# Weighted sum of attention values in a four-layer graph network: group updates in pieces, shared roots, and a mark on ScalarE

## What is computed

```python
h = jnp.maximum(_layernorm(x, axis=-1), 0.0)
x = x + _L0_gnn_ref(h, src, dst, ...)     # inside it:
    e = jnp.exp(score - smax[dst])
    m = v[src] * (e / ssum[dst])[:, :, None]
    t = jax.ops.segment_sum(m, dst, num_segments=N).reshape(N, DIM)
    new_h = (t @ Wa + ba) * alpha + h * (1.0 - alpha)
h = jnp.maximum(_layernorm(x, axis=-1), 0.0)   # needs the inverse root of each node's variance
```

## Time and profile before

| | us |
|---|---|
| median of three runs | 10655.52 |
| profiled execution | 10607.1 |
| its span, first to last instruction | 10605.0 |
| weighted sum, first L1063 to last L1063 | 1544.9 to 1901.9 |
| busy in the span: PE, DVE, ACT, POOL | 5675.4, 3028.2, 949.0, 6216.3 |

### The profile page before, as it was taken

How to read it: one execution, slowest core, us unless ns; L and a number is a source line. 1 busy time by engine, 2 the same in 40 slices (tenths; PEclk the granted TensorE clock), 3 DMA queues, 4 the chain that set the end, 5 groups by cost and what they waited for, 6 DMA issues and landing times.

```text
span 10605.0 us, 107124 instructions
## 1 busy us (share of the span) xinstructions
PE 5675.4 (54%) x23750; PEld 3922.0 (37%) x23751; DVE 3028.2 (29%) x7366; ACT 949.0 (9%) x1767; POOL 6216.3 (59%) x6738
## 2 busy tenths in 40 slices
PE   3566637566775667656675666653334333333334
PEld 2333437333443334433343333333333333333234
DVE  3444577212221122312222122331122112231222
ACT  1111100111111111101111111110000000000000
POOL 3655536565555655466554655546666666656665
PEclk7566659777887788878788778875566556665666
DMA  5777755332323323233332323221111111111111
GB/s 167 218 219 218 203 139 155 90 88 82 85 75 86 87 82 85 79 85 87 83 83 75 88 81 81 77 59 45 47 49 48 46 46 49 48 46 46 47 49 47
DMA packets 796948, 945.08 MB, mean 89 GB/s; under 512 B 269045, under 2 KB 530448, under 8 KB 796302
## 3 DMA queue, kind: packets, MB, share of 16 engines
q0 software_dynamic: 213408, 463.35, 16.4%
q1 hardware_dynamic: 474970, 390.60, 13.2%
q10 hardware_dynamic: 108436, 89.99, 2.6%
HBM read 797.55 MB, written 152.25 MB: 90 GB/s over the span
## 4 chain that ended last, share of the span: by engine, by line
another core or an unknown queue 44%; PE 18%; issue 13%; DVE 9%; DVEq 3%; POOL 0%; SPq 0%; ACT 0%; DMA 0%; ACTq 0%; POOLq 0%
PE ps_big L1119 8%; PE ps_seg L1126 5%; DVE onehots L1715 2%; DVE sums L1746 2%; DVEq L453 1%; PE ps_seg L1197 1%; PE ps_big L1197 1%; PE ps_big L1063 1%; PE ps_t L1038 1%; DVE gate L1894 1%; DVE h_res L1898 0%; DVE group_stats L1783 0%; PE ps_seg L1063 0%; PE ps_big L987 0%
## 5 line engine op out<-in xcount | busy, mean ns | idle before, releaser
L871 POOL DMA_INDIRECT rows<-node_rows,idx_all x5488 | 5209.8, 949 | 3470.5 <-SPq L713 1590.0
L1119 PE MATMUL ps_big<-rows,ident 128*128 (+1 forms) x1960 | 1221.8, 709 | 1386.0 <-DVE onehots L1715 1249.5
L1746 DVE TENSOR_TENSOR sums<-sums,ps_seg 128x128 f32 x1342 | 385.5, 287 | 5141.3 <-remote 3368.8
L1126 PEld LDWEIGHTS ps_seg<-onehots 128*128 128x128 f32 x7840 | 1206.0, 223 | 899.0 <-issue 735.5
L1126 PE MATMUL ps_seg<-onehots 128*128 128x128 f32 x7840 | 1236.4, 309 | 260.6 <-issue 168.0
L1715 DVE SCALAR_TENSOR_TENSOR onehots<-ps_mm,away 128x512 f32<-128x512 f32 x1975 | 1349.3, 684 | 21.4 <-issue 13.8
L1197 PE MATMUL ps_seg<-rows,onehots 128*128 (+1 forms) x2952 | 613.8, 372 | 1235.4 <-DVE onehots L1715 595.8
L1119 PE MATMUL ps_big<-q_res,ident 128*128 (+1 forms) x1960 | 1153.9, 674 | 150.9 <-issue 123.0
L1119 PEld LDWEIGHTS ps_big<-rows,ident 128*128 128x128 f32 x1960 | 412.0, 224 | 2036.2 <-DVE onehots L1715 1461.7
L871 POOL DMA_INDIRECT sums<-kv_rows,idx_all x784 | 743.4, 948 | 548.2 <-SPq L711 281.2
L1197 PEld LDWEIGHTS ps_seg<-rows,onehots 128*128 128x128 f32 x2952 | 536.7, 272 | 1301.7 <-DVE onehots L1715 619.0
(11 more groups left out here) (215 smaller groups left out, 2974.4 us busy)
## 6 DMA issues: line engine op xcount, KB each, us to landing
q_res<-gates_by_edge SPq DMA_DIRECT2D x784, 256.0 KB
rows<-node_rows,idx_all POOLq DMA_INDIRECT x5488
rows<-dst_padded SPq DMA_DIRECT2D x196, 256.0 KB
value_rows_by_edge<-sums SPq DMA_DIRECT2D x196, 256.0 KB
gates_by_edge<-gate ACTq DMA_DIRECT2D x196, 256.0 KB
rows<-value_rows_by_edge SPq DMA_DIRECT2D x196, 256.0 KB, 3.5
node_rows<-h_res ACTq DMA_DIRECT2D x49, 448.0 KB
sums<-kv_rows,idx_all POOLq DMA_INDIRECT x784
```

The lines of the kernel that those rows point to most:

```text
L871: pool.indirect_dma_start(target[:, r, j, :], None, table, bass.IndirectOffsetOnAxis(ap=idx_all[:, c * J + j:c * J + j + 1], axis=0), elem ...
L1119: last = nc.tensor.matmul(ps_big[u][:, :], ident[:, :], chunk_words(source, slot, 0, CHUNK), start=n == 0, stop=n == 1)
L1126: last = nc.tensor.matmul(ps_seg[u][:, 0:D], onehots[:, u, j, :], msg[:, u, j, 0:D], start=j == 0, stop=j == J - 1)
L1746: V.tensor_tensor(mine, mine, seg_four[(n - 1) % depth][:, 0:D], ALU.add).then_inc(agg_added, 1)
```

## The change

The update of a group that has ended is spread over three turns instead of two: VectorE divides at the end of the first, adds to x at the end of the next (not after n=3), and in the one after that takes the statistics of four windows after n=2, of three after n=3, and gathers them at the end, with a copy into a table for all windows (`mv`). The inverse root is taken once for groups 0 to 2 and once for groups 3 to 5, both inside the loop where the groups are far enough, and once for group 6. ScalarE finishes and stores groups 0 to 2 when groups 3 to 5 end, and groups 3 to 6 after its loop. The inverse root itself has 12 instructions instead of 13, here and in all later layers. The table has two more columns, for which SyncE issues four more DMAs. Step 4i+4 is marked by ScalarE at the beginning of its turn i: four Abs of a 128x128 row of numbers against the distance, and one Relu over 128x512; VectorE's n=2 then only adds.

```diff
-        SUM_WORDS, ROW_WORDS = 8, 12
+        SUM_WORDS, ROW_WORDS = 10, 12
-        WORD_LOADS = 11
+        WORD_LOADS = 15
+        ROOTS = ((0, 3), (3, 6), (6, 7))
+                    (sum_words[0:1, 0:1, 8:9], by_turn(ENDS_, 0, 1)[:, 0:1]),
+                    (sum_words[0:1, 1:TURNS_, 8:9], by_turn(ENDS_, 0, 1)[:, 0:TURNS_ - 1]),
+                    (sum_words[0:1, 0:1, 9:10], by_turn(ENDED_, 0, 1)[:, 0:1]),
+                    (sum_words[0:1, 1:TURNS_, 9:10], by_turn(ENDED_, 0, 1)[:, 0:TURNS_ - 1]),
...
-                        sum_weighted(slot, n % 4, onehot_ready, marked[n - 1])
+                        sum_weighted(slot, n % 4, onehot_ready if n < UNROLL else fourth_ready, marked[n - 1])
...
+            def mark_fourth(i):
+                first = i * (UNROLL * J) + UNROLL * J
+                act.wait_ge(segsum_ready, i * UNROLL + 1)
+                for j in range(J):
+                    act.lower_ap(away[:, ds(first + j, 1)])
+                for j in range(J):
+                    last = nc.scalar.activation(onehots[:, 0, j, :], iota_f[:, :], ACT.Abs, bias=away[:, ds(first + j, 1)], scale=-1.0)
+                last.then_inc(distance_ready, 1)
+                act.wait_ge(distance_ready, i + 1)
+                nc.scalar.activation(onehots[:, 0, :, :], onehots[:, 0, :, :], ACT.Relu, bias=1.0, scale=-1.0)\
+                    .then_inc(fourth_ready, 1)
             def group_parts(i, words):
+                mark_fourth(i)
...
             def attend_group(g):
-                with act.If(g != 0):
-                    finish_and_store(one_before(g, GROUPS))
+                with act.If(g >= LATER), clamped(act, [g - LATER], 0, LATER - 1) as earlier:
+                    finish_and_store(earlier[0], 0)
...
             each_turn(act, "act", row_words, slice(10, 12), group_parts)
-            finish_and_store(GROUPS - 2)
+            finish_and_store(LATER, 1)
             copy_group(0, GROUPS - 1, copies_u)
-            finish_and_store(GROUPS - 1)
+            for g in range(LATER + 1, GROUPS - 1):
+                finish_and_store(g, 1)
+            finish_and_store(GROUPS - 1, 2)
...
-                do(V.tensor_scalar(v, x, add, None, ALU.add))
+                do(V.tensor_scalar(v, x, add, 0.5, ALU.add, ALU.mult))
...
-                do(V.tensor_scalar(v, v, -0.5, None, ALU.mult))
...
+            def gather_attention(g):
+                wait_alone(dve, "dve", group_chain[0], g * OPS_ATT + 3)
+                for i in range(GROUP):
+                    last = V.bn_aggr(group_mv[:, i, :], group_stats[:, i, :])
+                last.then_inc(group_chain[0], 1)
+                wait_alone(dve, "dve", group_chain[0], g * OPS_ATT + 4)
+                V.tensor_copy(mv[:, ds(g * GROUP, GROUP), :], group_mv[:, :, :]).then_inc(group_chain[0], 1)
+            def finish_attention(g):
+                gather_attention(g)
+                for n, (_, end) in enumerate(ROOTS[:-1]):
+                    with dve.If(g == end - 1):
+                        take_roots(n)
...
                     V.tensor_tensor(mine, mine, seg_four[(n - 1) % 4][:, 0:AGGW], ALU.add).then_inc(agg_added, 1)
-                    mark_step(at, (n + 2) % 4)
-                    if n == 3:
-                        with dve.If(words[4] != 0), clamped(dve, words[5:6], 0, GROUPS - 1) as group:
-                            add_attention(group[0])
+                    if n != 2:
+                        mark_step(at, (n + 2) % 4)
+                    if n == 2 or n == 3:
+                        with dve.If(words[8] != 0), clamped(dve, words[9:10], 0, GROUPS - 1) as group:
+                            sample_attention(group[0], *STATS[n - 2])
                 with dve.If(words[4] != 0), clamped(dve, words[5:6], 0, GROUPS - 1) as group:
+                    add_attention(group[0])
+                with dve.If(words[8] != 0), clamped(dve, words[9:10], 0, GROUPS - 1) as group:
                     finish_attention(group[0])
```

More of the change, by code:

```diff
@@ L1067, in attend_steps @@
             def attend_steps(i, words):
-                marked = [pe.compute_val(i * UNROLL + (N_ONEHOT + 1 + n)) for n in range(1, UNROLL + 1)]
+                marked = [pe.compute_val(i * (UNROLL - 1) + (N_ONEHOT + 1 + n)) for n in range(1, UNROLL)] + [i + 1]
                 with clamped(pe, words[5:5 + UNROLL], 1, CHUNKS) as counts:
@@ L1354, in group_parts, with finish_and_store @@
                             attend_group(group[0])
-            def finish_and_store(g):
-                wait_alone(act, "act", deviation_ready, g + 1)
+            def finish_and_store(g, roots):
+                act.wait_ge(deviation_ready, roots + 1)
                 for i in range(GROUP):
@@ L1360, in finish_and_store @@
                                                 x_res[:, ds(g * GROUP + i, 1), :].rearrange("p w d -> p (w d)"), ACT.Relu,
-                                                bias=group_nmr[:, i:i + 1], scale=group_rstd[:, i:i + 1])
+                                                bias=nmr[:, ds(g * GROUP + i, 1)], scale=rstd[:, ds(g * GROUP + i, 1)])
                 last.then_inc(group_done, 1)
-                wait_alone(act, "act", group_done, g + 1)
-                act.sem_inc(deviation_used, 1)
                 store_group(0, g, 0)
+            LATER = ROOTS[0][1]
             def attend_group(g):
-                with act.If(g != 0):
-                    finish_and_store(one_before(g, GROUPS))
-            act.sem_inc(deviation_used, 1)
+                with act.If(g >= LATER), clamped(act, [g - LATER], 0, LATER - 1) as earlier:
+                    finish_and_store(earlier[0], 0)
             act.wait_ge(words_loaded, 16 * WORD_LOADS)
+            act.wait_ge(away_loaded, 16)
             nc.scalar.copy(agg[:, :, :], zero_col[:, :].rearrange("p (a b) -> p a b", a=1)
@@ L1451, in inverse_root @@
                     do(V.tensor_tensor(t, t, v, ALU.mult))
-                    do(V.scalar_tensor_tensor(y, t, 1.5, y, ALU.add, ALU.mult))
+                    do(V.scalar_tensor_tensor(y, t, 1.5, y, ALU.subtract, ALU.mult))
             dve.wait_ge(dst_loaded, 96)
@@ L1867, in _ @@
                 mark_step(n * J, n)
-            each_turn(dve, "dve", sum_words, slice(0, 8), attend_steps)
+            each_turn(dve, "dve", sum_words, slice(0, 10), attend_steps)
+            regs = [dve.alloc_register(f"dve_last_{next(load_no)}")]
+            dve.load(regs, sum_words[0:1, TURNS_ - 1:TURNS_, 4:5].rearrange("a i n -> a (i n)"))
+            with dve.If(dve.snap(regs[0], donate=True) != 0):
+                for part_ in STATS:
+                    sample_attention(GROUPS - 2, *part_)
+                gather_attention(GROUPS - 2)
+                take_roots(1)
+            for r in regs:
+                dve.free_register(r)
             add_attention(GROUPS - 1)
-            finish_attention(GROUPS - 1)
+            for part_ in STATS:
+                sample_attention(GROUPS - 1, *part_)
+            gather_attention(GROUPS - 1)
+            take_roots(2)
             inverse_root(chain, dinv[:, :], agg[:, :, D + HEADS], 1.0, root_all[:, 0, :], root_all[:, 1, :])
```

39 lines of the change are left out of this document (21 added, 18 removed).

## The result

The changed kernel took 10772.4 us (median of 4 runs, 10745.6 to 10792.8), the kernel before 10649.9 beside it (4 runs): a ratio of 1.012, 95% interval 1.0092 to 1.0149. It is 122 us slower, where the prediction had it 22 us faster and its range ended at 10670. On another chip the ratio was 1.0131 (1.0116 to 1.0145).

What follows compares the result with a forecast made beforehand. Weighted sum bound by transfers early, then by mark cycles between VectorE and TensorE plus group updates; terms -22 - 1 + 4 - 3 + 0 = -22 us, 10655.5 to 10633, range 10600 to 10670.

Steps and rivals of the forecast that it cites:

- loop's end 0.9: VectorE's time at the end of a weighted-sum turn, taken as 0.9 us in the group walk and the plain-turn cycle.
- The regime bound by transfers: Weighted sum, step 0 and first 20 turns, 4.8 us each: transfers bound them, so relief for VectorE brings nothing.
- two cycles: Plain turns of the weighted sum: a short cycle through step 4i+4's mark, 4.1 us, and one over two turns, 8.6.
- ScalarE's mark: Weighted sum's plain turns: ScalarE marking step 4i+4 takes 2.55 us, turns go from 4.32 to 4.28, 1 us saved.
- Group updates in pieces: Six groups updated in the weighted sum's loop: each costs 8.2 us instead of 13.9, 5.8 saved per group.
- deep relief: Rival: VectorE's pieces vanish in its spare time, 9 us saved a group, 42 in all, time 10613; chance 0.17.
- pieces that hold marks: Rival: pieces bring branches and stretched instructions, a group costs 11 us, roots 7 each, time 10655; chance 0.27.
- Two roots in the loop: Inverse roots at turn ends in the weighted sum: 5 us each plus 1 for TensorE's restart, 12 us back.
- plain turns above 4.6 (ScalarE): Sign that would show the forecast wrong: weighted-sum plain turns longer than 4.6 us, with ScalarE as the cause.
- Four more table loads: SyncE's added DMAs for the table: 4 us lost, range 2.7 to 5.3, zero if pass 0 recovers.
- After the loop: ScalarE finishes groups 4 and 5 in idle time before group 6's scale: 0 us change, just fitting.
- The shorter root of the later passes: One instruction less in each of 42 roots in passes 2 to 7: 3 us saved, range zero to 9.

Runs made afterwards that it cites:

- rows of 10 against 12: Changed kernel with all four marks on VectorE, sums table of 10 words a row against 12: ratios 1.017 and 0.9989 to the kernel before.
- the fastest kernel: Changed kernel, 8-word rows, VectorE keeping last turn's words 4 and 5 in registers, three end-of-turn conditions inside one: 10619.1 us, ratio 0.9954.
- rows of 12: Changed kernel with the sums table at 12 words a turn instead of 10, the last two unused: 10498.2 us against 10506.2, ratio 0.9989.
- the four kernels with ScalarE's mark and aligned tables: Changed kernel with 12-word rows, 10 loaded (0.9989) or 12 loaded (0.998); with 8-word rows and two words kept in registers (0.9968), plus joined conditions (0.9954).
- carried words: Changed kernel with 8-word rows and 11 table loads, VectorE keeping last turn's words 4 and 5 in two registers: 10624.7 us against 10663.1, ratio 0.9968.
- carried words and one branch: As carried words, with the three conditions at the end of VectorE's turn inside one: 10619.1 us, ratio 0.9954 to the kernel before.
- TensorE's table off: Kernel before with the table of the rows, which TensorE loads, starting two words (8 bytes) later: ratio 1.0112, 119 us slower.

## Why the prediction was wrong

*The sum left out the load.* The step that failed is that two terms were carried from the old kernel into the new one as if nothing touched them: VectorE's "loop's end 0.9", in the walk of a group and in the cycle of a plain turn, and TensorE's "2.0" from mark to first step. Both hold a register load whose length depends on the table's layout, and the diff changes the layout in its first line. The prediction counted the added words as DMAs (four table loads) and not as what reads them, 60 times on VectorE, and did not ask who else reads the table. With that, 0.85 became 2.87 on TensorE and 0.60 became 1.06 and 2.30 on VectorE. It cost 183 us with the marks on VectorE (rows of 10 against 12, one chip). For the change as it stood it was about 149 us, by 1.0131 against 0.9989 on two chips.

*The regime bound by transfers has no slack for a longer turn.* The prediction had it that relief for VectorE brings nothing in the first 20 turns. That holds: 97.2 us in the fastest kernel, 96.8 before. But the longer loads raised the same turns from 4.8 to about 7 us, half of the stretch's loss.

*The aligned rest was also mis-sized, and a cycle was missing.* With rows of 12, plain turns are 4.72 and not 4.28. The prediction walked two cycles, and neither is the one that binds here: add and mark, TensorE's third step, add and mark, and VectorE's idle time at the loop's end, all within one turn. A plain turn less that idle time is the same in the four kernels with ScalarE's mark and aligned tables: 4.72 - 1.62, 4.50 - 1.41, 4.31 - 1.22 and 4.01 - 0.92 are 3.1 each. With the old 0.9 this cycle is 4.0 and hides behind the other two; with ten words instead of eight (0.46 more) and one more branch at the loop's end and one more inside the turn it leads. The prediction had "some 0.3 of branches" once per group and none in a plain turn. Carrying the words took 0.4 off the turn, joining the branches 0.1 to 0.3 more.

*Group updates in pieces: nearly right.* Three turns of the first group, from 1638.05 to 1660.22, in the kernel with rows of 12:
```profile
1638.05 0.30 DVE L1891 TENSOR_TENSOR sums<-sums,ps_seg 128x137 f32 x1 [1.62 <-PE ps_seg L1069]
...
1649.11 1.26 DVE L1841 SCALAR_TENSOR_TENSOR x_res<-ps_t,alpha,x_res 128x512 f32 x2
1652.91 0.30 DVE L1891 TENSOR_TENSOR sums<-sums,ps_seg 128x137 f32 x1 [2.53 <-issue]
...
1655.51 0.67 DVE L1849 BATCH_NORM_STATS2 group_stats<-x_res 128x6 f32 x3
...
1660.22 0.30 DVE L1891 TENSOR_TENSOR sums<-sums,ps_seg 128x137 f32 x1 [2.34 <-issue]
```
22.17 less three plain turns of 4.72 is 8.0. With carried words the second group costs 8.5 in the same way (5.81 + 8.68 + 6.96 less three of 4.32), but the first one 11.0 (6.45 + 10.52 + 6.98). The forecast was 8.2, where the prediction read 13.9 from the earlier trace rows. Over all six groups, roots included, the 40 turns stand 59 us above plain ones with rows of 12 and 67 with carried words; the forecast was 62, the kernel before 84. So deep relief (4 a group) did not come, and the 11 of pieces that hold marks came only in that first group.

*Two roots in the loop: somewhat better.* The turns with a root and their next ones cost 4.4 and 3.3 us extra with rows of 12, 3.9 and 5.1 with carried words; forecast 6 each. The first chain on 21 elements a partition, changed kernel:
```profile
1826.81 0.18 DVE L1469 TENSOR_SCALAR root_all<-mv 128x21 f32<-128x21 f32 x1
...
1827.70 0.98 DVE L1474 TENSOR_TENSOR root_all<-root_all 128x21 f32<-128x21 f32 x1
...
1830.23 0.18 DVE L1867 SCALAR_TENSOR_TENSOR nmr<-mv,rstd 128x21 f32<-128x21 f32 x1
```
It took 3.6 us with one instruction of 0.98 in it. The first chain before, on 7 elements, took 6.2 with two instructions more and four of 0.89 to 0.98; others before took 4.8 to 6.4, and the second one with rows of 12, without any such instruction, 2.8. An ordinary instruction takes 0.18 where it took 0.17, so the width costs next to nothing, as said; most of the gain is fewer stretched instructions, and what stretches them is not shown.

*ScalarE's mark: right in mechanism, priced too dear.* The length c is 2.26 and not 2.55. By the prediction's own cycle a turn is (4.0 + 2.26 + 2.0) / 2 = 4.13, and 4.01 to 4.2 came once the loop's end was short: the mark brought 8 us instead of 1. The figures of the Trainium skill ("ScalarE: Activation LUTs", What ACT_TABLE_LOAD costs), by which the four Abs were an estimated 1.27, agree with the 1.27 and 1.28 of the trace; the 1.4 that the prediction took from the rows of two pointer operands does not. Its rule to use VectorE for relu (Rules for kernel authors) did not hold here, where VectorE's queue is on the cycle: 337.3 us against 345.6. The sign "plain turns above 4.6 (ScalarE)" did come, with 4.72 and 9.0, but without ScalarE's mark the turns were no shorter.

*Four more table loads: as dear to issue as forecast, lost in the scatter.* Fifteen took SyncE 19.95 us (forecast 19), eleven 14.63:
```profile
165.84 19.95 SPq L764 DMA_DIRECT2D early<-step_words_by_field  x15
```
Pass 0 ended at 1426.8 to 1445.6 in the six profiles with 15 or 17 loads, and at 1427.8 to 1452.1 in the eight with 11. A cost of 4 us is neither shown nor excluded.

*After the loop: right.* ScalarE finishes groups 4 and 5 (2.80 each from 1989.31 and 1993.50) and stands for 1.04 us before the last one's scaling, where the earlier trace rows had 9.13. From the last matmul of the weighted sum to the first of the second layer it is 29.9 us in both kernels.
```profile
1993.50 2.80 ACT L1380 ACTIVATE h_res<-x_res,nmr,rstd 128x128 f32<-128x128 f32 x7
...
1998.81 2.80 ACT L1380 ACTIVATE h_res<-x_res,nmr,rstd 128x128 f32<-128x128 f32 x7 [1.04 <-DVE nmr L1867]
```
The shorter root of the later passes (3 us) was not measured by itself. Nor is it settled why the kernel with carried words and one branch gains 49 us in the whole and 20 in the weighted sum: the interval of the whole is 30 to 67, and the kernel before was not profiled beside it on that chip.

## What to carry to other kernels

When a change adds a word to a table, look at every engine that reads the table or one behind it, and at what its rows start on: a register load sits in an engine's queue, counts as no busy time, shows as "issue" idle or is put down to an engine that was long done, and is repeated in every turn. Keep rows and starts on multiples of 16 bytes, and pad a load to whole fours of words. Price the loop's end of each engine anew, load and branches, before any work inside the turn: here it was worth more than everything that the change set out to move. Walk the cycles that are slightly shorter than the one that binds, too: a few tenths at the loop's end made one of them lead.

## What the runs showed of the hardware

Register loads (TENSOR_LOAD) from a table in SBUF, length of one: starting on a multiple of 16 bytes, 8 words 0.60, 10 words 1.06, 12 words 0.85 us; starting 8 bytes off it, 8 words about 1.86, 10 words 2.30, 12 words 2.87. Two words are 0.49 to 0.50 either way (ScalarE). One of 12 words can so be faster than one of 10, and a shift by 8 bytes made one 3.4 times as long. Starts 4 bytes off were not tried.

Of the extra time in TensorE's queue only a part is lost. With TensorE's table off, 61 · 2.02 = 123 us of longer loads made the weighted sum 91.5 us longer. The second layer, with four times as many, took 5201 us against 5164 and 5175 of the two aligned kernels on that chip. The some 184 loads in the convolutions cost nothing that the profiles show (3488 against 3485 and 3486).
